# A hand-ordered attention and recurrent-cell kernel: all engines' orders and the load order rewritten

## What is computed

```python
y = einsum('bnh,boh->bno', x, W[itok_7]) + b[itok_7]            # a weight matrix for each sequence
q, k, v = y @ Wq.T + bq, y @ Wk.T + bk, y @ Wv.T + bv            # 16 heads
sim = einsum('bhid,bhjd->bhij', q, k) / sqrt(16) / temp
scores = sum(alpha[h, f] * sin(2 * pi * sim / freq[f] + phi[h, f]) for f in range(5))
w = sigmoid(scores); w = w / (sum(w, -1) + 1e-10)
x = x + layernorm((w @ v) @ Wo.T + bo) * gamma + beta
h = relu(x @ W1[itok_8] + b1[itok_8]) @ W2[itok_8] + b2[itok_8]  # an adapter for each sequence
z = layernorm(x + h) * gamma2[itok_8] + beta2[itok_8]
for t in range(32):                                              # a recurrence over the 32 sequences
    f = sigmoid(z[t] @ wf.T + c @ uf.T + bf); i = sigmoid(z[t] @ wi.T + c @ ui.T + bi)
    g = tanh(z[t] @ wc.T + c @ uc.T + bc);    c = f * c + i * g
x = x + tanh(z @ wo.T + c @ uo.T + bo)
```

## Time and profile before

| | before |
|---|---|
| median of 3 runs | 320.94 us (320.41 to 322.8) |
| profiled execution, its own time | 323.39 us |
| its span, first to last instruction | 321.6 us |
| PE busy | 285.4 us (89%) |
| DVE busy | 274.6 us (85%) |
| ACT busy | 257.3 us (80%) |
| POOL busy | 51.6 us (16%) |
| mean granted TensorE clock | 0.983 |

### The profile page before, as it was taken

One profiled execution on the slowest core, in us unless ns is written; L12 is line 12 of the kernel. 1 busy time (PEld: TensorE's weight loads), 2 busy tenths in 40 slices (PEclk: granted clock), 3 DMA queues, 4 the chain that ended last, 5 costly groups with the idle time before them and its releaser, 6 DMA issues.

```text
span 321.6 us, 7374 instructions
## 1 busy us (share of the span) xinstructions
PE 285.4 (89%) x2686; PEld 177.5 (55%) x2686; DVE 274.6 (85%) x598; ACT 257.3 (80%) x378; POOL 51.6 (16%) x58
## 2 busy tenths in 40 slices
PE   0787898969889989999999998899999999998971
PEld 0576647866546855554575645556665545543350
DVE  3049996999999999999999998999999998554265
ACT  1069998999999999999999999899999894422132
POOL 5000600041100012332100214140013331210000
PEclk9999997998999999999999999999999999999997
DMA  5698427544044248045445240330444160020007
GB/s 174 244 388 303 93 30 227 116 135 67 0 91 117 30 113 242 0 75 118 103 88 143 74 68 1 71 70 15 108 106 67 35 150 16 2 34 2 0 0 261
DMA packets 32374, 31.97 MB, mean 99 GB/s; under 512 B 10706, under 2 KB 24274, under 8 KB 32338
## 3 DMA queue, kind: packets, MB, share of 16 engines
q1 hardware_dynamic: 27410, 26.67, 29.1%
q0 software_dynamic: 4352, 4.20, 8.7%
q10 hardware_dynamic: 576, 0.64, 0.8%
HBM read 23.36 MB, written 2.10 MB: 79 GB/s over the span
## 4 chain that ended last, share of the span: by engine, by line
DVE 39%; PE 32%; ACT 14%; issue 8%; DMA 3%; POOL 2%; SPq 1%; DVEq 0%; ACTq 0%; POOLq 0%
DVE sc L1626 12%; PE pg L694 7%; DVE ang L1615 5%; PE pg L685 5%; DVE ang L1606 5%; ACT ang L1130 4%; PE pf L491 3%; PE pav L589 3%; ACT ang L1139 3%; PE pf L571 2%; PE pf L547 2%; DVE fc L1761 2%; ACT sc L1121 2%; DMA w<-x 1%; DVE vz L1596 1%
## 5 line engine op out<-in xcount | busy, mean ns | idle before, releaser
L1139 ACT ACTIVATE ang<-ang,qs 128x2560 f32<-128x2560 int32 x32 | 77.4, 2433 | 0.3 <-DVE ang L1615 0.2
L1626 DVE SCALAR_TENSOR_TENSOR sc<-ang,ratio,sc 128x512 f32<-128x512 f32 (+1 forms) x120 | 73.0, 637 | 0.4
L1130 ACT ACTIVATE ang<-sc,phase 128x512 int32<-128x512 f32 (+1 forms) x110 | 64.5, 650 | 0.0
L685 PE MATMUL pg<-gate_w,zT 128*64 128x384 f32 x256 | 50.8, 499 | 0.6 <-DVE zT L1751 0.4
L694 PE MATMUL pg<-gate_u,cT 128*64 128x384 f32 x256 | 47.7, 493 | 1.6 <-DVE cT L1770 1.5
L1615 DVE TENSOR_SCALAR ang<-ang 128x2560 int32<-128x2560 int32 x32 | 47.5, 1501 | 0.0
L1606 DVE TENSOR_SCALAR ang<-sc,phase 128x256 int32<-128x256 f32 (+1 forms) x90 | 32.4, 412 | 2.6 <-ACT sc L1121 2.5
L1179 ACT ACTIVATE gat<-pg 128x384 f32<-128x384 f32 x32 | 15.6, 487 | 22.7 <-PE pg L694 22.3
L694 PEld LDWEIGHTS pg<-gate_u,cT 128*64 128x64 f32 x256 | 16.4, 136 | 22.1 <-issue 15.0
L513 PE MATMUL pf<-wc,xg 128*64 128x256 f32 x128 | 17.1, 416 | 9.5 <-DMA wc<-in_cond 8.8
L1149 ACT ACTIVATE sc<-sc,lead 128x512 f32<-128x512 f32 (+1 forms) x40 | 23.4, 628 | 2.3 <-DVE sc L1626 2.2
(11 more groups left out here) (114 smaller groups left out, 474.1 us busy)
## 6 DMA issues: line engine op xcount, KB each, us to landing
wc<-in_cond SPq DMA_DIRECT2D x30, 257.0 KB, 3.5
w<-in_up SPq DMA_DIRECT2D x32, 128.5 KB, 2.6
wa<-in_down SPq DMA_DIRECT2D x32, 66.0 KB, 1.9
xt<-in_xt SPq DMA_DIRECT2D x8, 256.0 KB, 3.0
xt<-rows POOLq DMA_DIRECT2D x8, 256.0 KB, 4.2
w<-x POOLq DMA_DIRECT2D x8, 256.0 KB, 4.2
xg<-in_x SPq DMA_DIRECT2D x3, 512.0 KB, 5.1
qm<-qT SPq DMA_DIRECT2D x48, 32.0 KB, 2.1
```

Source lines behind the costliest of these rows:

```text
L685: pe.matmul(pg[n % 2][u * L:(u + 1) * L, 0:GCOLS], zT[:, q % 2, kc, t * L:(t + 1) * L], gate_w[:, kc, u, :], start=False, stop=(kc == KC - ...
L1130: op = act.activation(ang[:, n % SLOTS, f, r], unit(n)[:, r], ACT.Identity, scale=TURN / FREQS[f], bias=phase[:, p * NF + f:p * NF + f + 1])
L1139: act.activation(a.bitcast(F32), a, ACT.Sin, scale=2 * PI_LOW / TURN, bias=qs[:, 3:4]).then_inc(sine_ready, 1)
L1626: op = dve.scalar_tensor_tensor(out=unit(n)[:, r], in0=ang[:, n % SLOTS, f, r].bitcast(F32), scalar=ratio[:, p * NF + f:p * NF + f + 1], i ...
```

## The change

Only tables and the order of steps change; every step computes what it did.

- Five frequencies of a unit are shared out by `ON_ACT`: units 10, 12 and 21 give one angle each from ScalarE to VectorE, unit 22 gives one back.
- `BIAS_BY_PE` has 15 cells where it had 14 (13, 21 and 28 come in, 17 and 24 go out), `ROW_BY_PE` has part 6 too, so that no `output_row(6)` runs.
- SyncE asks for the attention constants right behind wq and wk, then for group 1, and for the nine rest constants behind that.
- All five lists are in another order. The `warm` matmuls are 64 where they were 63, in other places.

```diff
-ON_ACT = [1, 2, 3, 1, 3, 4, 1, 4, 3, 4, 2, 4, 2, 3, 3, 4, 3, 4, 3, 3, 3, 3, 3, 3, 3, 4, 3, 4, 2, 3, 3, 2]
+ON_ACT = [1, 2, 3, 1, 3, 4, 1, 4, 3, 4, 1, 4, 1, 3, 3, 4, 3, 4, 3, 3, 3, 2, 4, 3, 3, 4, 3, 4, 2, 3, 3, 2]
-BIAS_BY_PE = (0, 1, 2, 4, 6, 8, 10, 12, 14, 16, 17, 18, 24, 31)
-ROW_BY_PE = (0, 1, 2, 3, 4, 5)
+BIAS_BY_PE = (0, 1, 2, 4, 6, 8, 10, 12, 13, 14, 16, 18, 21, 28, 31)
+ROW_BY_PE = (0, 1, 2, 3, 4, 5, 6)
...
             sp.dma_start(wk[:], wk_in).then_inc(qk_s, 16)
-            load_rest_consts()
             load_attention_consts()
+            load_cond(1, 2)
             load_x(1)
+            load_cond(1, 0)
             load_cond(1, 1)
             load_cond(1, 3)
-            load_cond(1, 0)
-            load_cond(1, 2)
+            load_rest(1, 0)
+            load_rest_consts()
...
             input_gates(27, 1)
+            gate_bias(28)
+            state_turned(26)
             turn_normed(7)
-            state_turned(26)
             state_gates(27)
```

More of the change, by code:

```diff
@@ L764, in _ @@
             weighted(1)
+            turn_output_row()
             scores(3)
+            warm(3)
             weighted(2)
[L767 removed]
             weighted(3)
[L769 to L770 removed]
             values(1, 0)
@@ L774, in _ @@
             values(2, 1)
+            turned(0)
+            warm(9)
             output_bias(0)
@@ L878, in _ @@
+            state_turned(5)
+            weighted(15)
             input_gates(6, 1)
-            state_turned(5)
             input_gates(7, 0)
+            state_gates(6)
+            scores(11)
+            output_part(1, 1)
+            output_part(2, 0)
+            values(5, 0)
+            gate_bias(8)
+            state_turned(6)
             input_gates(7, 1)
-            values(5, 0)
-            state_gates(6)
+            state_gates(7)
+            weighted(16)
+            weighted(17)
@@ L1226, in _ @@
             keys(0, 1)
+            angle(0, 4)
+            copy_scores(2)
+            copy_scores(3)
             angle(1, 3)
             angle(1, 4)
-            copy_scores(2)
-            copy_scores(3)
             sines(0, False)
-            first_biases()
-            halved(0)
             angle(2, 2)
@@ L1242, in _ @@
             queries(1, 0)
-            halved(1)
+            sines(3, False)
             keys(1, 0)
-            sines(3, False)
             queries(1, 1)
-            keys(1, 1)
             weights(0, True)
             weights(1, False)
+            keys(1, 1)
+            halved(0)
+            halved(1)
             copy_scores(4)
             copy_scores(5)
+            first_biases()
             weights(2, False)
+            copy_scores(6)
             weights(3, False)
-            copy_scores(6)
             copy_scores(7)
@@ L1262, in _ @@
             angle(5, 4)
+            sines(4, True)
+            turned(0)
             angle(6, 4)
-            turned(0)
-            sines(4, True)
-            squares(0)
             sines(5, False)
@@ L1269, in _ @@
             copy_scores(8)
+            angle(7, 1)
             copy_scores(9)
-            angle(7, 1)
             angle(7, 2)
-            residual_turned(0)
+            squares(0)
             copy_scores(10)
+            copy_scores(11)
             angle(7, 3)
             angle(7, 4)
-            copy_scores(11)
             angle(8, 2)
@@ L1298, in _ @@
             angle(11, 4)
+            queries(2, 0)
+            keys(2, 0)
+            sines(9, False)
             sines(10, False)
@@ L1951, in _ @@
             moments(1, 0)
+            add_sine(14, 1)
             moments(1, 1)
+            add_sine(14, 2)
+            state_copy(2)
+            wrap(16)
+            normalise(1)
             conditioned(3)
-            add_sine(14, 1)
-            add_sine(14, 2)
+            residual(2)
+            modulated(1)
+            residual_added(2)
             add_sine(15, 0)
-            normalise(1)
+            cell_step(3, 0)
+            add_sine(15, 1)
+            cell_step(3, 1)
+            angle(17, 0)
@@ L1986, in _ @@
+            cell_step(4, 1)
+            divided(6, 2)
             add_sine(16, 3)
+            normalise(2)
+            state_copy(4)
+            wrap(18)
+            add_sine(17, 0)
+            wrap(19)
+            cell_step(5, 0)
+            add_sine(17, 1)
+            cell_step(5, 1)
+            modulated(2)
+            state_copy(5)
+            add_sine(17, 2)
             divided(7, 0)
-            cell_step(4, 1)
-            normalise(2)
+            add_sine(18, 0)
+            shifted_language(2)
```

748 lines of the change are left out of this document (354 added, 394 removed).

## The result

The changed kernel takes 325.02 us (median of 20 runs, 322.46 to 326.96) against 321.58 for the kernel before beside it (20 runs, 319.3 to 324.15): ratio 1.0108, 95% interval 1.0078 to 1.0138. It is **slower by 1.1 per cent**. The forecast was 320.8 us with a range of 318.2 to 324.2, and the measured median lies 0.8 us above it. (The kernel before measured 0.64 us more than the 320.94 that the forecast started from; as ratios, the range ends at 1.0102 and 1.0108 was measured. The value, no change at all, missed clearly.) The profiled execution of the changed kernel took 326.03 us, span 324.2 (before 323.39 and 321.6).

A forecast was written before the change was run, and what follows sets the result against it. VectorE, the fullest of three nearly full engines from 60 to 270 us, was taken as the bound. Terms 0.7 - 1.6 + 1.9 - 0.9 - 0.25 = -0.15 put 320.94 at 320.8 us, range 318.2 to 324.2.

The forecast's parts named there:

- VectorE's start: Up to group 1's yT: nothing won by the new order; with the angle shares, +0.7 us remains.
- the steps of both lists up to yT: Start: VectorE's steps add to 18.0 us in each kernel, so both reach group 1's yT at 37.6.
- Shares between engines: VectorE takes two more angles net, +0.8 us where it is full; ScalarE's and TensorE's changes cost nothing.
- From 38.8 to 60 us: VectorE's waits of 0.90 and 1.43 us shrink to 0.7 us of waits in place of 2.33: -1.6 us.
- From 60 to 80 us: VectorE newly waits for ScalarE and for GpSimd's root: +1.9 us, bounds 0 and +3.
- The two waits forecast at 72 to 76 us: VectorE waits 1.1 us at angle(8, 0) for ScalarE, then 0.9 at residual(0) for GpSimd's root.
- the change doesn't do what it says: Rival, chance 0.05: spread_q(1, 1) delays group 2's condition loads past 75 us; three us late cost 2, giving 322.8.
- the other rival: Chance 0.07: TensorE's clock falls after new waits between 62 and 72 us, slowing group 2's conditions: 323.6 or 324.5.
- Middle: More VectorE work between squares and residual in parts 3 to 7 removes the wait at 199.58: -0.9 us.
- VectorE waits anew in each group: Rival, chance 0.08: group 1's 1.9 us of waits recurs in groups 2, 3 and 4, giving 326.5.
- the signs by which the prediction called itself wrong: Middle: VectorE idle over 5 or under 1.5 us, or not the full engine; or TensorE's clock falling after 70 us.
- End: Last cells: gate_bias(24) leaves full TensorE for idle ScalarE, a last turn moved costs perhaps 0.2: -0.25 us.

The follow-up runs named there:

- e1_warm: The changed kernel with two warm matmuls put back ahead of the first queries: 323.45 us, ratio 1.004 to the kernel before.
- e3_both: The changed kernel with two warm matmuls back ahead of the first queries and group 2's last two condition loads asked for earlier: 322.48 us, ratio 1.0013.
- e5_before_less_warm: The kernel before without its two warm matmuls ahead of the first queries: 322.13 us, ratio 1.0007.
- e12_on_act: e3_both with the angles shared between VectorE and ScalarE as in the kernel before: 322.81 us, ratio 1.0044.
- e2_loads: The changed kernel with group 2's last two condition loads asked for ahead of spread_q(1, 1): 324.48 us, ratio 1.0068.
- e15_filled_gap: The changed kernel with warm(6) ahead of condition(4, 0), the loads staying late: 323.65 us, ratio 1.003.
- e14_before_mended: The kernel before with warm(9) at the very start and the rest constants asked for behind group 1's condition loads: 322.26 us, ratio 0.9996.
- e11_before_early_warm: The kernel before with warm(9) at the very start alone: 319.61 us, ratio 0.9966.
- e17_longer_warm: e16_after_mended with warm(13) in place of warm(9) at the very start: 319.18 us, ratio 0.9885.
- e6_early_warm: e3_both with warm(9) at the very start, ahead of condition(0, 0): 321.7 us, ratio 0.9989.
- e10_all: e6_early_warm with six small moves in VectorE's order around the waits for GpSimd's roots: 322.89 us, ratio 1.0045.
- e16_after_mended: e6_early_warm with three small moves in VectorE's order ahead of residual(1), normalise(1) and normalise(4): 321.03 us, ratio 0.9961.

## Why the prediction was wrong, point by point

- **VectorE's start (+0.7 in all).** `centre_output_weights` stood at 18.26 us with no wait for a DMA, as forecast. But `yT` of group 1 came at 38.26 and not at 37.6. The step that failed is the adding of "the steps of both lists up to yT": it took the first copied scores as given at 21.06. The warm matmuls that the change removes ahead of the first queries got no term at all: they stood at nothing without a reason. They are worth about 2 us in the new order (e1_warm, e3_both) and nothing in the old (e5_before_less_warm).
- **Shares between engines (+0.8).** The busy time of the angles of width 512 grew by 1.0 us (19.5 to 20.5), but the sum over VectorE did not (274.6 and 274.5), and giving the angles back won nothing (e12_on_act).
- **From 38.8 to 60 us (-1.6).** Right in kind and too small: both waits, 2.33 us together, went and no new one above 0.2 us came in that trace. (The wait of 0.5 us for ScalarE's copies, forecast at 54, is there in e3_both, whose start is early: 0.53 at 53.08.) What the prediction missed is that the two waits had been slack for a late start.
- **From 60 to 80 us (+1.9).** The two waits forecast at 72 to 76 us were 0.22 together; ScalarE was some 1.0 us ahead of the prediction's sum of it (`squares(0)` done at 72.34 and not at 73.3). In their place came 1.50 us at `hidden(0)`.
- **The loads.** The rival "the change doesn't do what it says" named `spread_q(1, 1)` and asked when the last condition load is issued: 72 by the prediction's count, 69.88 to 73.57 for the last four in the trace. It got 0.05 since it was priced by lateness alone: "one microsecond late costs nothing, three cost 2". The wait of 2.29 us brought a fallen clock, the other rival's mechanism; the two were one, and together they were worth about 1 us in the median (e2_loads, e3_both) or more (e15_filled_gap).
- **Middle (-0.9).** This is the step that failed by most: VectorE's waits for roots grew by 3.9 us where 0.9 was to go. It expected more distance between `squares` and `residual`. In the traces the time from the end of `squares` to VectorE's coming for the root did not grow, 1.9, 1.6 and 1.5 us before for parts 3, 4 and 5 and 1.6, 1.9 and 1.4 after, and half of the new waits stand there, 2.4 us. It left out the distance from `moments` to `normalise`, where the other half stands, which in VectorE's work went from 3.1 to 2.4 us for part 1 and from 4.6 to 1.9 for part 0. And it counted VectorE's work as time for GpSimd, whatever the work was: a wrap in the window gives GpSimd nothing. The wait at 199.58 went, and eight of 0.2 to 0.9 us came. The rival "VectorE waits anew in each group" (0.08, 326.5) had the right pattern with another cause. Two of the signs by which the prediction called itself wrong came: VectorE idled for 7.41 us in the middle, over 5, and TensorE's clock fell after 70 us.
- **End (-0.25).** Measured -0.07 in idle time; too small to tell.

Each cause has its experiment: start about 2 us, roots about 2.4, loads about 1, against 2.3 won at 49 to 57 us. Clear of the noise are the start, the start and the loads together (3.1 us), and the roots; the loads alone are seen in the traces and not surely in the medians. The terms add to 3.1, near the 3.4 measured, but each is sure to 1 to 2 us only, so this sum is a check of size and no exact account. Open is how much of its early start e14_before_mended had over its twelve runs (in its trace a third), and how often the clock rises late; a trace shows one execution at a time.

## What to carry to other kernels

Before booking a removed wait as a gain, ask what it was slack for: the work ahead of it becomes the limit, with all its variance. Treat warm matmuls as steps with a price, above all where TensorE's clock has not risen yet, and fill TensorE's idle time at the very start. And count a helper engine's time by what the busy engine does beside it, not by how much.

## What the runs showed of the hardware

- GpSimd's operation on 128x2 takes 0.21 us and the power behind it, the second operation of a root, 0.72 beside a VectorE step that reads PSUM (134.12 in the kernel before), 0.25 and 0.71 beside angles (239.91 there); beside wraps of 1.49 us they take 1.71 and 2.02.
- The granted clock reads 1.00 from 8 to 20 us in most traces although the first 16 condition matmuls take 3.68 us, against 1.95 where TensorE has worked ahead of them. At the start the column hides the low level (1.2 and not 2.4 GHz); only durations of one form show it. The Trainium skill (TensorE: Matmul & The Clock Gate, Part 1: The HAM clock gate) has the throttled level as the default one, and the early warm matmuls agree.
- Behind TensorE's waits of 0.70, 0.72 and 1.09 us for loads the clock stayed; behind 2.00 us, 2.21 (e11_before_early_warm, group 1) and 2.29 (twice) it fell. Ahead of the first conditions, behind early warm matmuls, it stayed at waits of 1.34, 1.81, 1.93 and 2.07 us (e17_longer_warm, e6_early_warm, e10_all, e11_before_early_warm) and fell at 2.09 and 2.66 (e16_after_mended, e14_before_mended). One wait of 2.00 us fell and one of 2.07 stayed, so the length of the wait alone does not decide it.
